# Attention with a following expert layer: where PSUM is emptied, full banks for the row maxima, masks by matmul, three P buffers and the rotary partner by DMA

## The reference

```python
# x (4, 1024, 256): B = 4 batches, T = 1024, C = 256; H = 16 heads, L = 64, DH = 16
q_lat = (x @ Wq_down).reshape(b, t, H, L)          # k_lat, v_lat alike
q_c, q_e = einsum(q_lat, Wq_up_c), einsum(q_lat, Wq_up_e)   # 8 dimensions each; k alike
v = einsum(v_lat, Wv_up)
q = concatenate([q_c, rope(q_e)]); k = concatenate([k_c, rope(k_e)])
att = softmax(where(causal, q @ k.T / 4, -inf))
x = layernorm(x + (att @ v).transpose.reshape @ Wc)
# experts: E = 8, FF = 512, two of eight by Sinkhorn-normalised gates (3 iterations)
out = sum over the two best of gate * (relu(x @ wg[e]) * (x @ wp[e])) @ wo[e]
x = layernorm(2 * x + out)
# rope(x) = x * cos + rot * sin, where rot swaps each even dimension with the odd one behind it
```

## Time and profile before

| | us |
|---|---|
| median of 3 runs (lowest, highest) | 1464.13 (1461.82, 1464.49) |
| profiled execution, device time | 1461.37 |
| its span, first to last instruction | 1459.6 |

### The profile page before, as it was taken

One profiled execution on the slowest core, in us unless ns is written; L12 is line 12 of the kernel. 1 busy time (PEld: TensorE's weight loads), 2 busy tenths in 40 slices (PEclk: granted clock), 3 DMA queues, 4 the chain that ended last, 5 costly groups with the idle time before them and its releaser, 6 DMA issues.

```text
span 1459.6 us, 18976 instructions
## 1 busy us (share of the span) xinstructions
PE 1176.3 (81%) x5806; PEld 665.3 (46%) x5806; DVE 878.0 (60%) x2287; ACT 655.2 (45%) x1060; POOL 612.9 (42%) x629
## 2 busy tenths in 40 slices
PE   4558888888888888788888766479999998999880
PEld 2323333333333333343343322138878876887760
DVE  1456656666655565655576575026665695568886
ACT  1114445444444444444443323265556655566553
POOL 2213332232333333333223217633454447569884
PEclk8656579569878667778677555589999999999995
DMA  9603044215304314303302265401111112223335
GB/s 307 87 1 44 23 70 73 34 40 102 48 27 70 51 40 86 48 26 52 46 15 31 29 199 202 134 22 42 46 44 51 51 45 87 64 68 95 94 95 173
DMA packets 74691, 104.49 MB, mean 72 GB/s; under 512 B 12192, under 2 KB 58976, under 8 KB 74464
## 3 DMA queue, kind: packets, MB, share of 16 engines
q1 hardware_dynamic: 68448, 86.48, 26.3%
q0 software_dynamic: 6144, 16.79, 3.7%
HBM read 44.41 MB, written 33.03 MB: 53 GB/s over the span
## 4 chain that ended last, share of the span: by engine, by line
PE 56%; DVE 16%; POOL 10%; issue 6%; SPq 4%; ACT 4%; DMA 2%; POOLq 0%; ACTq 0%; DVEq 0%
PE X L689 11%; PE O L722 10%; PE S L790 10%; PE X L809 6%; PE S L708 5%; DVE X L1017 5%; DVE mx L1015 4%; POOL xs L1301 3%; PE X L671 3%; PE X L745 3%; POOL yn L1328 3%; POOL WL L1314 2%; DMA KQ<-ph 2%; PE X L680 2%; ACT P L856 2%
## 5 line engine op out<-in xcount | busy, mean ns | idle before, releaser
L856 ACT ACTIVATE P<-S 128x1024 f32<-128x1024 f32 (+3 forms) x384 | 301.2, 810 | 413.9 <-PE S L708 411.9
L1017 DVE CUSTOM_DVE_ANT_0 X<-X,MQ 128x128 f32<-128x128 f32 (+3 forms) x512 | 242.3, 515 | 187.7 <-PE X L689 186.0
L689 PE MATMUL X<-KQ 48*128 48x512 f32 (+3 forms) x768 | 216.9, 553 | 137.0 <-DVE mx L1017 89.2
L1287 POOL TENSOR_SCALAR_AFFINE_SELECT P<-P 128x256 f32<-128x256 f32 x256 | 103.0, 407 | 369.8 <-ACT P L856 367.9
L1314 POOL TENSOR_TENSOR WL<-W,WH 128x1024 fp32r<-128x1024 f32 x78 | 186.6, 2392 | 165.7 <-ACT WH L911 165.3
L689 PEld LDWEIGHTS X<-KQ 48*128 48x128 f32 x768 | 101.0, 243 | 332.5 <-DVE mx L1017 126.6
L722 PE MATMUL O<-P,V 128*17 128x512 f32 (+3 forms) x1536 | 218.5, 652 | 41.7 <-POOL P L1287 40.9
L1015 DVE TENSOR_REDUCE mx<-X 128x1 f32<-128x512 f32 x256 | 164.7, 685 | 87.2 <-PE X L689 86.3
L708 PE MATMUL S<-KQ 50*128 50x512 f32 (+3 forms) x768 | 178.1, 474 | 6.5 <-DMA KQ<-mb 4.6
L911 ACT CAST WH<-W 128x1024 fp32r x156 | 163.0, 1046 | 16.9 <-issue 16.4
L809 PE MATMUL X<-W,hT 128*128 x624 | 147.9, 380 | 1.5 <-ACT ot L924 0.9
(11 more groups left out here) (147 smaller groups left out, 1472.4 us busy)
## 6 DMA issues: line engine op xcount, KB each, us to landing
KQ<-ph SPq DMA_DIRECT2D x128, 128.0 KB, 4.6
xs<-zt SPq DMA_DIRECT2D x78, 128.0 KB, 1.9
xg<-xs SPq DMA_DIRECT2D x78, 128.0 KB, 2.2
ys<-ot SPq DMA_DIRECT2D x78, 128.0 KB, 1.7
KQ<-pl SPq DMA_DIRECT2D x64, 128.0 KB, 6.2
XT<-xT SPq DMA_DIRECT2D x4, 1024.0 KB, 8.6
x<-x SPq DMA_DIRECT2D x1, 4096.0 KB, 23.5
W<-wg SPq DMA_DIRECT2D x8, 512.0 KB, 9.8
```

The costliest lines, as they stand in the source:

```text
L689: e.matmul(b[:, 0:k1 - k0], KQ[u % 3][rows, 0, p, qb * 128:qb * 128 + 128].bitcast(f32r), KQ[u % 3][rows, 1, p, k0:k1].bitcast(f32r), star ...
L856: e.activation(P[:, pr, g % 2, :, 0:w], S[pr][:, :, 0:w], ACT.Exp, scale=0.25).then_inc(act_p, 1)
L1017: t = e.tensor_tensor_reduce(b[:, 0:w], b[:, 0:w], MQ[:, 512 - w:512], 1.0, NEG, ALU.add, ALU.max, mx[:, u % 2, i, 1:2])
```

## The change

Projections, values and the transposes of y (but those of the last batch) no longer take X banks. They take one of the two halves S[0], S[1], in turn with the scores (`sjob`, `claim_half`; one semaphore act_s counts what ScalarE has emptied). Values and transposes are made two tiles at a time. The X banks are left to what VectorE empties. The maxima's 24 pieces per unit become 18 full banks of 512 columns (BANKS), some with two pieces; all are reduced by tensor_reduce. The diagonal's mask is added in PSUM by two bf16 matmuls per diagonal block, with tables BM; each of the two heads claims its bank by itself. The final reduction becomes two, the negation and splitting two operations instead of three. P gets a third buffer, and value products run two steps late, also across units. The shuffle is replaced by 8 DMAs per chunk from SP (the rotary dimensions are permuted so that partners are 8 rows apart); ph and pl share the memory of tr and t1. The maxima's lane begins 600 columns earlier. The last two of the 24 weight blocks are loaded after attention.

```diff
 STEPS = [(q, kb) for q in range(2) for kb in range(4 * q + 4)]
-MAXES = [(p, qb, k0, min((qb + 1) * 128, k0 + 512)) for p in range(2) for qb in range(8)
-         for k0 in range(0, (qb + 1) * 128, 512)]
+
+ROWS = (0, 2, 4, 6, 1, 5, 3, 7)
+BANKS = (([(7, 0, 512, 0)], 28, 1), ([(7, 512, 1024, 0)], 29, 1), ([(6, 0, 512, 0)], 15, 1),
+         ([(4, 512, 640, 0), (6, 512, 896, 128)], 11, 4), ([(5, 0, 512, 0)], 23, 1),
+         ([(1, 0, 256, 0), (5, 512, 768, 256)], 18, 4), ([(4, 0, 512, 0)], 8, 1), ([(3, 0, 512, 0)], 24, 1),
+         ([(0, 0, 128, 0), (2, 0, 384, 128)], 3, 4))
+MAXES = [(p, *bank) for p in range(2) for bank in BANKS]
...
             add("v", b, i)
-            job("v", b, i)
-            emptied("A", "v", b, i)
-            yield 0.5
+            sjob("v", b, i)
+            yield 1
 
     def maxima(u):
-        for n, (p, qb, k0, k1) in enumerate(MAXES):
+        for n in range(len(MAXES)):
             add("m", u, n)
             for a in range(2):
                 job("m", u, n, a)
             for a in range(2):
                 emptied("D", "m", u, n, a)
...
         for n, (q, kb) in enumerate(STEPS):
             w = 512 - max(0, kb * 128 - q * 512)
             for pr in range(2):
                 add("s", u, n, pr)
+                sjob("s", u, n, pr)
                 spread(cols + (0.35, 0.484)[pr] * w)
             turn_out()
-            if late is not None:
-                pv(late)
+            if len(late) == 2:
+                values_product()
             cols += w
-            late = n
+            late.append((u, n))
             spread(cols)
-        pv(late)
-        spread(4608)
 
     def turn_out():
...
         if u + 1 < NU:
-            lanes[1].add(("m", u + 1), maxima(u + 1), 27, U * u - 300 * (u > 0), U * (u + 1) - 300)
+            lanes[1].add(("m", u + 1), maxima(u + 1), 19.1, U * u - 900 * (u > 0), U * (u + 1) - 900)
...
+        def half(*key):
+            return S[pl_.score[key] % 2]
+
+        def claim_half(q, *key):
+
+            k = pl_.score[key]
+            if k >= 2:
+                q.wait_ge(act_s, k - 1)
+            return half(*key)
+
+        def scored(*key):
+            return pl_.score[key] + 1
...
+                if kind == "pj" and a[2] == 1:
+                    u, ch, phase = a
+                    q.wait_ge(act_s, scored("pj", u, ch))
+                    if u:
+                        q.wait_ge(d_kq[(u - 1) % 3], 192 * ((u - 1) // 3 + 1))
+                    else:
+                        q.wait_ge(dve_init, 2)
+                    for row in range(16, 128, 32):
+                        e.dma_start(tr[row:row + 8, ch, :], tq[row + 8:row + 16, ch, :]).then_inc(d_sw[ch], 16)
+                        e.dma_start(tr[row + 8:row + 16, ch, :], tq[row:row + 8, ch, :]).then_inc(d_sw[ch], 16)
+                elif kind == "pd":
...
                         e.dma_start(W[:, i * 1024:i * 1024 + 1024].rearrange("p (k f) -> p k f", f=w),
                                     src[i // 3].rearrange("(k p) f -> p k f", p=128)).then_inc(d_fw, 16)
-                    loaded = 20
+                    loaded = 18
                 elif kind == "moe":
                     q.wait_ge(pe_pv, 192)
                     q.wait_ge(pe_x, at["x", "ot", 15, 1])
+                    for i in range(22, 24):
+                        src, w = ((wg, FF), (wp, FF), (wo, C))[i % 3]
+                        e.dma_start(W[:, i * 1024:i * 1024 + 1024].rearrange("p (k f) -> p k f", f=w),
...
-                    for kt in range(2):
-                        t = e.matmul(b[:, 0:264], XT[n % 2][:, kt, i * 128:i * 128 + 128], WE[:, kt, 512:776], start=kt == 0, stop=kt == 1)
-                    t.then_inc(pe_x, 1)
+                    for h in range(2):
+                        j = 256 * i + 128 * h
+                        for kt in range(2):
+                            t = e.matmul(b[:, h, 0:264], XT[n % 2][:, kt, j:j + 128], WE[:, kt, 512:776], start=kt == 0, stop=kt == 1)
+                    t.then_inc(pe_s, 1)
                 elif kind == "m":
                     u, n = a
-                    p, qb, k0, k1 = MAXES[n]
-                    two = [claim(q, "m", u, n, h) for h in range(2)]
+                    p, segments, slot, many = MAXES[n]
                     q.wait_ge(d_kq[u % 3], 192 * (u // 3 + 1))
-                    for h, b in enumerate(two):
-                        rows = slice(64 * h, 64 * h + 48)
-                        e.matmul(b[:, 0:k1 - k0], KQ[u % 3][rows, 0, p, qb * 128:qb * 128 + 128].bitcast(f32r),
-                                 KQ[u % 3][rows, 1, p, k0:k1].bitcast(f32r),
-                                 start=True, stop=True).then_inc(pe_x, 1)
+                    q.wait_ge(dve_init, 2)
+                    for h in range(2):
+                        b = claim(q, "m", u, n, h)
+                        rows, both = slice(64 * h, 64 * h + 48), slice(64 * h, 64 * h + 64)
+                        for qb, k0, k1, c in segments:
+                            c1, edge = c + k1 - k0, k1 == (qb + 1) * 128
+                            t = e.matmul(b[:, c:c1], KQ[u % 3][rows, 0, p, qb * 128:qb * 128 + 128].bitcast(f32r),
+                                         KQ[u % 3][rows, 1, p, k0:k1].bitcast(f32r), start=True, stop=not edge, skip_group_check=True)
+                            if edge:
+                                e.matmul(b[:, c1 - 128:c1], BM[both, 0, :], BM[both, 2, :], start=False, stop=False, skip_group_check=True)
+                                t = e.matmul(b[:, c1 - 64:c1], BM[both, 1, :], BM[both, 3, 64:128], start=False, stop=True, skip_group_check=True)
+                        t.then_inc(pe_x, 1)
                 elif kind == "mt":
...
                     w = width(n)[3]
-                    q.wait_ge(pe_s, 2 * g + pr + 1)
-                    if g >= 2:
-                        q.wait_ge(pe_pv, g - 1)
+                    q.wait_ge(pe_s, scored("s", u, n, pr))
+                    if g >= 3:
+                        q.wait_ge(pe_pv, g - 2)
                     elif g == 0:
                         q.wait_ge(pe_x, at["x", "rw2"])
-                    e.activation(P[:, pr, g % 2, :, 0:w], S[pr][:, :, 0:w], ACT.Exp, scale=0.25).then_inc(act_p, 1)
+                    e.activation(P[:, pr, g % 3, :, 0:w], half("s", u, n, pr)[:, :, 0:w], ACT.Exp, scale=0.25).then_inc(act_s, 1)
                 elif kind == "oc":
...
-                            t = e.tensor_reduce(mx[:, u % 2, i, 0:1], b[:, 0:w], AX, ALU.max)
-                        else:
-                            t = e.tensor_tensor_reduce(b[:, 0:w], b[:, 0:w], MQ[:, 512 - w:512], 1.0, NEG, ALU.add, ALU.max,
-                                                       mx[:, u % 2, i, 1:2])
-                        t.then_inc(dve_x, 1)
+                        e.tensor_reduce(mx[:, u % 2, 2 * h + p, slot:slot + many], bank("m", u, n, h).rearrange("p (n k) -> p n k", n=many),
+                                        AX, ALU.max).then_inc(dve_x, 1)
...
-                        q.wait_ge(act_x, at["f", "pj", u, ch])
+                        q.wait_ge(act_s, scored("pj", u, ch))
                         q.wait_ge(d_c, 80)
                         if u:
-                            q.wait_ge(pool_rope, at["D", u - 1, ch])
+                            q.wait_ge(d_kq[(u - 1) % 3], 192 * ((u - 1) // 3 + 1))
                         e.tensor_tensor(t1[:, ch, :], tq[:, ch, :], RP[:, 0, cs], ALU.mult).then_inc(pool_rope, 1)
```

247 lines of the change are left out of this document (129 added, 118 removed).

## The result

| | us, median (lowest to highest) | ratio to before, 95% interval |
|---|---|---|
| before | 1464.31 (1461.82 to 1475.45) | |
| changed | 1424.65 (1415.56 to 1431.17) | 0.971 (0.963 to 0.980) |

The forecast was 1414.

The account below looks back on a forecast made before the run. Bank waits for the maxima and a 0.743 clock bound attention. Its 521 full-speed us become 566, at clock 0.88 643 us, 58 under 701; with +7.5, +4.5 and -4 that gives 1411, forecast 1414, range 1345 to 1510.

Parts of the forecast that it names:

- (1): Attention maxima in full banks claimed one by one: 85 full-speed us of waits go, 8 more from fewer pairs.
- Rival E: Attention maxima: no relief, as VectorE's own rate with the batch ends binds; 1462 within 5, chance 0.05.
- (2): Causal masks of the maxima on TensorE: 0.18 us per diagonal block, 75 full-speed us in units 0 to 12.
- Rival B: Masks on TensorE: weight loads stay in view, 0.36 us per block; 1516 us, chance 0.12.
- (3): Maxima's score tiles: a mask behind the first head's tile ends the heads' overlap in 10 of 18 pairs; 28 us.
- (4): Next unit's maxima 600 columns earlier: TensorE waits for KQ's landing, 4 us per unit, 45 full-speed us.
- (5): Projections, values, transposes through score halves: nothing; later value products with three P buffers save 10 full-speed us on POOL.
- (6): Rotary partner by DMA from SP's queue: nothing in the units, +7.5 us at the start.
- (7): Two of 24 weight blocks loaded after attention, ahead of the first xg on SP: +4.5 us.
- (8): Units 13 to 15: POOL's scatters still hold masks back; 4 us off for the maxima beside routing.
- Rival A: Attention clock stays low as the KQ wait brings the low level back; 1533 us at 0.74, chance 0.13.
- rival C: Attention gains more: clock to 0.95, cheapest masks, KQ wait 2 us; half of that is 575 us, whole 1346, chance 0.17.

Follow-up runs that it names:

- e2: Kernel before with the new maxima alone (full banks claimed one by one, masks on TensorE, maxima 300 columns ahead); 1351 us, ratio 0.916.
- e3: Changed kernel without the two mask matmuls behind each diagonal block, so maxima are taken without the causal mask; 1379 us, ratio 0.941.
- e11: e10 with both heads' banks claimed together and their tiles issued side by side, then their masks; 1369 us, ratio 0.925.
- e10: e6 with VectorE's shuffle for units 0 and 1 only, all weight blocks loaded early, former turns in the last batch's end; 1345 us, ratio 0.911.
- e8: Changed kernel with VectorE's shuffle in place of the swap DMAs, maxima still 900 columns ahead; 1411 us, ratio 0.966.
- e5: e4 with VectorE's shuffle in place of the swap DMAs; three P buffers and shared ph and pl stay; 1336 us, ratio 0.913.
- e4: Changed kernel with the next unit's maxima 300 columns ahead, as before the change, instead of 900; 1421 us, ratio 0.969.
- e7: e5 and e6 together: shuffle, two P buffers, products one step late, separate ph and pl, maxima 300 columns ahead; 1341 us, ratio 0.918.
- e6: e4 with ph and pl in their own memory, two P buffers and value products one step late, swap DMAs kept; 1343 us, ratio 0.919.
- e12: e5 with the former number of turns in the last batch's end (one yield line); 1348 us, ratio 0.913.
- e9: Changed kernel with 16 spare matmuls in front of the KQ wait of units 1 to 15; 1417 us, ratio 0.967.
- e1: Changed kernel with the former maxima: 24 pairs, two banks claimed at a time, masked on VectorE; 1551 us, ratio 1.056.

## Why the prediction held, and where it didn't

The direction came out (1425 against 1414) because the main step did. That the size did too is in part luck. In units 0 to 12 the masks were put 41 us too dear; against that stand a part of the other terms, the clock put too high (544 / 0.858 is 16 us more than 544 / 0.88), 5.5 us in units 13 to 15 and 6.8 us in the expert stage. By the prediction's parts:

- **(1) Maxima in full banks.** The step held: 91.9 us on VectorE fell to 7.2, under the 25 given. e2 shows that the new maxima alone, masks included, are worth 113 us, 98 of them in units 0 to 12, where 58 were forecast for everything. Rival E is out.
- **(2) Masks.** Mis-sized: 0.095 us per block by e3 instead of 0.18, 40 full-speed us instead of 75. That is 35 full-speed us, 35 / 0.858 = 41 in time, on the good side, and it is more than the 22 us by which full-speed time came out under 566. I had noted that the masks have half the passes of two transposes at 0.11 us each; half of 0.22 is 0.11, and I had gone above it to 0.18 without a row. Rival B is out. The Trainium skill's rule behind it ("TensorE: Matmul & The Clock Gate", "The mechanism"), by which a load overlaps only in other row groups, would leave both loads in view, and neither the rows at 265.71 and 265.78, 0.07 us apart with a load between them, nor e3 shows that.
- **(3) Lost pairing.** The size roughly held (e11). Its cause didn't: with the masks gone (e3) the loss stayed, and in e10 the heads run side by side with masks between them. It comes from claiming the banks one by one, which e11 undoes. Added up from the rows of units 0 to 12, each stretch taken with its clock, the full-speed sum went from 521 to 544 by -68 for the waits on VectorE, -12 for those on POOL, +46 for KQ and +57 for the starts of maxima, masks and scores.
- **(4) The maxima 600 columns earlier.** This is the step that failed, by its price and not by its length. The KQ wait is 4.05 us per unit, against 4, and about the 45 full-speed us that I counted. I also let it hold the clock at 0.88, but priced it by the 45 alone (45 / 0.88 = 51 us), and never asked what the clock would be without it. By e8 and e5, which differ in the 600 columns alone, they cost 75 us, 65 of them in units 0 to 12. Of these 7 are full-speed time, as other waits go with the 600 columns, and the rest is the clock, 0.837 instead of 0.918. Nor had I asked what the 600 columns were for: they keep the rows of the maxima ahead of the late swaps (e4), and without the swap they bring nothing.
- **(5) Score halves at nothing.** Right on cost (e7 against e2). The fall of the wait on POOL, which I credited to the later products, isn't shown to be theirs: with 300 columns it is 8.0 us in e5, with them, and 5.0 and 4.7 in e6 and e7, without them. With 900 columns (0.3 us) nothing was run without them.
- **(6) Rotary partner by DMA, at nothing in the units.** Beside the 900 columns that is so (e8). Taken by itself it isn't, and there the step missed something: at 300 columns swap and sharing together cost 61 us in units 0 to 12 (e4 against e5). I had noted that swaps and first products now wait for KQ's landing, and named what stood behind them on SP: the zeroing of xs. I left out the four issues of KQ<-mb, which the next scores need, and which e4 shows 3.4 to 6.8 us late. The changed kernel doesn't show that as a wait for rows, since its maxima come earlier; it pays for those in its place, under (4). The start-up, put at +7.5, was +9.9 against before; but e2 starts at 83.5, so the swaps cost 20 us there, and the new maxima had brought 10.
- **(7) Weight blocks.** +3.6 against +4.5.
- **(8) Units 13 to 15.** +1.5 against -4. I had left out that the masks are paid there too, at 0.57 of the clock. e3, without them, takes 166.2 us there instead of 171.4, but e4, with them, 164.4, so the cause stays open.
- **Not predicted: the expert stage, +6.8.** The batch's end has four yields less, and the last one is spread, with the second routing, over the expert tiles by the count of yields. "Its code hardly changes" was true of the experts and not of what runs between them (e10, e12).

**The clock.** 0.858 against 0.88. I had the right side, and e9 shows the cause: without standing for KQ it is 0.934. The Trainium skill ("TensorE: Matmul & The Clock Gate", "HAM oscillation — how this bites in real kernels") has bursts with waits on DMA between them start cold; the runs agree, 12 of 16 falls and the 0.076 of e9, though not in its strict form: at 0.743 the changed kernel would have taken 544 / 0.743 = 732 us there, and took 633.5. Rival A, which had c stay low, is out with it. (In rival C "half of that" doesn't fit its number: 575 us is 126 below 701, where half of 173 is 87.)

The largest miss is therefore in the account of the whole. The prediction held the change to be one gain with small costs. It is a gain of 113 us and two choices (900 columns; swap with shared buffers), either of which alone is enough to eat 75 to 85 us of what e5 has (e8, e4), while both together (the changed kernel) cost hardly more than one. The best versions found, e5, e12 and e10, stand at 0.911 to 0.913 of the time before, some 128 us under it, and 5 to 6% under the changed kernel; e6 and e7 can't be told from them.

## What to carry to other kernels

When a step is moved into a queue, list everything that later passes through this queue and who waits for it; here four small issues behind eight others, or the lead of the maxima that hides this, cost most of what the change's main part brought. A wait of 4 us once in a unit of 50 can cost more by the clock behind it than by its length. Take a change of many parts apart before judging it: two kernels, each with one half, showed what the total hid.

## What the runs showed of the hardware

**A clock bought with spare work.** 16 spare matmuls of 512 bf16 columns (15 of them recorded) took 3.40 us at 2.4 GHz in most units of e9, and units 0 to 12 became 25 us shorter.

**VectorE behind POOL.** In the changed kernel's second routing:

```profile
1118.80 0.23 DVE L1012 TENSOR_TENSOR rt<-rt,REV 128x64 f32<-128x64 f32 x1
...
1122.26 2.34 POOL L1359 TENSOR_TENSOR WL<-W,WH 128x1024 fp32r<-128x1024 f32 x1 [4.10 <-ACT WH L965]
1122.31 2.32 DVE L1016 TENSOR_SCALAR rs<-rs 128x8 f32<-128x8 f32 x1
...
1125.42 0.66 PE L818 MATMUL X<-rt,CST 128*128 128x64 f32 x2 [5.06 <-DVE rt L1214]
```

An operation on 8 columns took 2.32 us, ending with POOL's subtraction, where one on 64 columns took 0.23. TensorE stood 5.06 us behind it, and the clock was at 1.2 GHz from 1124.9 on for 6.8 us. The Trainium skill ("SBUF — State Buffer", "Who interferes with whom") says that the two engines share a pair of ports which one of them holds for a whole instruction; the row agrees. In e12 these small operations were held up just as long (2.1 to 2.4 us, six of them), but TensorE had other work, and the 5 us wait is gone. That is where the 6 us of the turns lie, as far as the traces tell; it was not tried by itself.

**A stop of several engines while rows are scattered.** In unit 14, beside POOL's 48 scatters, the waits of e9 to e12 have rows of a kind that no other kernel here has: "remote", a wait that nothing on this core ended. The longest of e10 and of e11, engine and line waited for, us in total, times, longest:

```profile
ACT P L902 <- remote: 24.1, 2, 22.3
DVE mx L1062 <- remote: 10.0, 2, 9.9
```

```profile
ACT P L906 <- remote: 26.2, 2, 25.8
DVE mx L1066 <- remote: 22.0, 4, 16.9
```

Units 13 to 15 took 178.4 to 188.1 us in these four kernels, 178.0 in e1 with the former maxima, and 164.4 to 171.4 in the others. What it is wasn't tried and stays open; by the record these four kernels also ran on other chips (6 and 7) than e1 to e8 (0 and 2), so that it may belong to the chip and not to the kernel. It spoils some 8 to 17 us of the profiled executions of e9 to e12, which is why I compared these by their stretches.
